# Attention worked off by pairs of steps, with one sum over the first two pairs of a region and GpSimd scaling 99 of 128 blocks

## What is computed

```python
q = (query @ Wq + bq).reshape(Bq, Sq, H, DK)      # Bq = 8, Sq = Sk = 512, H = 16, DK = 16
k = (key @ Wk + bk).reshape(Bq, Sk, H, DK)
v = (value @ Wv + bv).reshape(Bq, Sk, H, DK)
scores = jnp.einsum('bqhd,bkhd->hbqk', q, k) / np.sqrt(DK)
attn = jax.nn.softmax(scores.reshape(H * Bq, Sq, Sk), axis=0).reshape(H, Bq, Sq, Sk)
out = jnp.einsum('hbqk,bkhd->bqhd', attn, v).reshape(Bq, Sq, H * DK)
x = x + jnp.tanh(g_xattn[0]) * (out @ Wo + bo)
x = x + jnp.tanh(g_ffn[0]) * ffn(layernorm(x))
```

## Time and profile before

| what | value |
| --- | --- |
| time, median of 3 runs | 893.19 us (891.55 to 894.06) |
| time of the profiled execution | 890.11 us |
| its span, first to last instruction | 888.3 us |
| mean granted TensorE clock | 0.973 of 2.4 GHz |
| PE busy | 770.7 us (87%) |
| DVE busy | 781.0 us (88%) |
| ACT busy | 706.7 us (80%) |
| POOL busy | 494.9 us (56%) |
| `attend` | about 312 to 743 us |

### The profile page before, as it was taken

One profiled execution on the slowest core, in us unless ns is written; L12 is line 12 of the kernel. 1 busy time (PEld: TensorE's weight loads), 2 busy tenths in 40 slices (PEclk: granted clock), 3 DMA queues, 4 the chain that ended last, 5 costly groups with the idle time before them and its releaser, 6 DMA issues. The chain is left out here.

```text
span 888.3 us, 20668 instructions
## 1 busy us (share of the span) xinstructions
PE 770.7 (87%) x8127; PEld 438.8 (49%) x8149; DVE 781.0 (88%) x1001; ACT 706.7 (80%) x1095; POOL 494.9 (56%) x353
## 2 busy tenths in 40 slices
PE   8897887877777688999889999999999989948977
PEld 6563361112212155666556666666666657714434
DVE  4799539999999979999799999999999995767968
ACT  3454449999999878899788999999999952768973
POOL 1333463000000017999898999999999996514500
PEclk9999999999999989999999999999999989969999
DMA  9796786565555567778776786768857566200014
GB/s 299 262 315 203 245 240 130 138 167 140 140 139 130 202 183 228 239 225 265 231 227 211 234 265 191 212 174 259 259 164 211 168 225 192 91 1 1 0 43 148
DMA packets 98094, 164.34 MB, mean 185 GB/s; under 512 B 9616, under 2 KB 37008, under 8 KB 97680
## 3 DMA queue, kind: packets, MB, share of 16 engines
q1 hardware_dynamic: 98000, 163.03, 61.5%
HBM read 133.63 MB, written 41.94 MB: 198 GB/s over the span
## 5 line engine op out<-in xcount | busy, mean ns | idle before, releaser
L978 POOL TENSOR_TENSOR e<-e,recip 128x768 f32<-128x768 f32 (+3 forms) x256 | 387.4, 1558 | 34.6 <-DVE recip L1020 34.6
L928 ACT ACTIVATE e<-ps_att 128x512 f32<-128x512 f32 x512 | 302.0, 648 | 36.6 <-PE ps_att L869 35.6
L1009 DVE TENSOR_REDUCE pair_sums<-e 128x128 f32<-128x2048 f32 x128 | 291.6, 2281 | 20.0 <-ACT e L928 19.6
L869 PE MATMUL ps_att<-arena 128*128 128x128 bf16 x2048 | 192.7, 220 | 0.3 <-issue 0.2
L884 PE MATMUL acc<-e,arena 128*32 128x128 f32 x4096 | 179.5, 294 | 11.7 <-DVE e L990 4.2
L869 PEld LDWEIGHTS ps_att<-arena 128*128 128x128 bf16 x2048 | 151.0, 98 | 58.8 <-issue 3.6
L694 ACT ACTIVATE copies<-ps_max 128x1024 bf16<-128x1024 f32 x189 | 175.6, 1087 | 0.0
L865 PE MATMUL ps_att<-shift,minus 128*128 128x512 bf16 x394 | 154.2, 391 | 14.9 <-DMA arena<-k_stack 9.2
L884 PEld LDWEIGHTS acc<-e,arena 128*32 128x32 f32 x4096 | 106.6, 111 | 40.7 <-POOL e L978 10.9
L709 DVE TENSOR_TENSOR high<-copies,high 128x3072 bf16<-128x3072 bf16 x63 | 110.0, 1745 | 0.4 <-ACT copies L694 0.4
L961 POOL CAST bo_parts<-arena 96x256 bf16<-96x256 f32 x1 | 0.4, 394 | 175.5 <-DMA arena<-in_L_xattn_bo_dram 175.5
(11 more groups left out here) (162 smaller groups left out, 879.0 us busy)
## 6 DMA issues: line engine op xcount, KB each, us to landing
arena<-k_stack SPq DMA_DIRECT2D x256, 256.0 KB, 3.3
arena<-q_stack SPq DMA_DIRECT2D x64, 256.0 KB, 4.2
k_stack<-parts SPq DMA_DIRECT2D x40, 256.0 KB, 3.5
q_stack<-parts SPq DMA_DIRECT2D x40, 256.0 KB, 3.6
k_stack<-k_stack SPq DMA_DIRECT2D x12, 512.0 KB, 10.9
arena<-in_x_dram SPq DMA_DIRECT2D x5, 1024.0 KB, 8.7
arena<-in_ctx_dram SPq DMA_DIRECT2D x4, 1024.0 KB, 6.5
arena<-q_stack SPq DMA_DIRECT2D x8, 512.0 KB, 8.0
```

The costliest lines, as they stand in the source:

```text
L869: last = nc.tensor.matmul(bank[:, j * P:(j + 1) * P], ks[:, i % KRING, b * P:(b + 1) * P], qs[:, h, b * P:(b + 1) * P], start=False, stop= ...
L928: nc.scalar.activation(e_at(qc * STEPS + i, half * HB, (half + 1) * HB).rearrange("p q b i -> p b q i"), ps[(qc * (2 * STEPS) + 2 * i + ha ...
L978: nc.gpsimd.tensor_tensor(part, part, by_pairs(recip[:, kc % 2, :], share), ALU.mult).then_inc(pool_scaled, 1)
L1009: nc.vector.tensor_reduce(pair_sums[:, :, h // 2, :], e[:, g % RING // 2].rearrange("p q s b i -> p q i (s b)"), AX.X, ALU.add).then_inc(s ...
```

## The change

All lists of `attend` except SyncE's now go by pairs. PE computes the four halves of scores of a pair and then the product of both steps of the pair 10 before it. Before, the product of one step stood behind every two halves. The ring has 11 slots of a pair, which is the same memory. DVE sums pairs 0 and 1 of a region with one instruction, unless the two do not lie beside each other in the ring, and each other pair with one; it adds up seven partial sums. DVE and GpSimd each scale a whole pair with one instruction. GpSimd takes 9, 13, 13, 13, 13, 12, 13, 13 of the 16 blocks of the eight pairs, 99 of 128, and 6 of 16 in the last region. DVE scales a pair 8 pairs after its sum's place in the list. The gathers stand behind pairs 4, 6, 8 and 10 of a chunk of queries.

```diff
-    LAG = 20
-    SLAG = 17
-    RING = 22
+    LAG = 10
+    RING = 11
+    GATHER_AT = [LAG - PAIRS + BANK_PAIRS * (j + 1) for j in range(BANKS)]
-        return 7 if i % 4 == 1 else 6
+    POOL_BLOCKS = (9, 13, 13, 13, 13, 12, 13, 13)
+    END_BLOCKS = 6
+    GROUPS = ((0, 1), (2,), (3,), (4,), (5,), (6,), (7,))
...
 TensorE
-                    for i in range(STEPS):
-                        for half in range(2):
-                            scores(qc, i, half)
-                        if LAG <= i < LAG + H and (i - LAG) % BANK_HEADS == 0:
...
-                        if i >= LAG or not first:
-                            for half in range(2):
-                                times_v(qc * STEPS + i - LAG, half)
+                    for j in range(CHUNK):
+                        for half in range(4):
+                            scores(qc, 2 * j + half // 2, half % 2)
+                        if LAG <= j < LAG + PAIRS and (j - LAG) % BANK_PAIRS == 0:
+                            bank = (j - LAG) // BANK_PAIRS
+                            if not first:
+                                pe.wait_ge(gathered, BANKS * (qc - 1) + bank + 1)
+                            clear(bank)
+                        if j >= LAG or not first:
+                            times_v(qc * CHUNK + j - LAG)
...
 ScalarE
+                        if p >= RING:
+                            act.wait_ge(multiplied, p - RING + 1)
+                        for half in range(4):
+                            n = 4 * p + half
+                            act.wait_ge(scored, n + 1)
...
 GpSimd
+                for p in range(ALL_PAIRS):
+                    r = p // PAIRS
+                    if p % PAIRS == 0:
+                        pool.wait_ge(recip_ready, r + 1)
+                    share = pool_share(p)
+                    part = e_at(p, 0, share)
+                    nc.gpsimd.tensor_tensor(part, part, by_pairs(recip[:, r % 2, :], share), ALU.mult
+                                            ).then_inc(pool_scaled, 1)
...
 VectorE
+                def add_up(p, n, k):
+                    dve.wait_ge(exped, 4 * (p + n))
+                    t = p % RING
+                    nc.vector.tensor_reduce(partial[:, :, k, :], e[:, t:t + n].rearrange("p t q z i -> p q i t z"),
+                                            AX.XY, ALU.add).then_inc(sum_done, 1)
...
+                for r in range(NC * NC):
+                    for k, (p, n) in enumerate(groups(r)):
+                        if r:
+                            if k == 0:
+                                dve.wait_ge(sum_done, groups_before(r) + r)
+                            if p % PAIRS < PAIRS - 1:
+                                for i in range(n):
+                                    scale(p + i - PAIRS)
+                                if p % PAIRS + n == PAIRS - 1:
+                                    scale(p + n - PAIRS)
+                        add_up(p, n, k)
+                    invert(r, len(list(groups(r))))
+                for p in range(ALL_PAIRS - PAIRS, ALL_PAIRS):
+                    scale(p)
```

More of the change, by code:

```diff
@@ L746, in attend, with pool_share, groups, groups_before @@
     STORE_AT = 26
-    GATHER_AT = [LAG - H + BANK_HEADS * (j + 1) + 2 for j in range(BANKS)]
+    BANK_PAIRS = BANK_HEADS // 2
+    GATHER_AT = [LAG - PAIRS + BANK_PAIRS * (j + 1) for j in range(BANKS)]
     Q_STEPS = {STEPS - H + h + 2 * h // 3: h for h in range(H)}
[L751 to L755, removed]
-        return 7 if i % 4 == 1 else 6
-    FIRST_PRESET = 2 * LAG + 3
+    POOL_BLOCKS = (9, 13, 13, 13, 13, 12, 13, 13)
+    END_BLOCKS = 6
+    GROUPS = ((0, 1), (2,), (3,), (4,), (5,), (6,), (7,))
+    def pool_share(p):
+        return END_BLOCKS if p >= ALL_PAIRS - PAIRS else POOL_BLOCKS[p % PAIRS]
+    def groups(r):
+        for group in GROUPS:
+            p = r * PAIRS + group[0]
+            if len(group) == 2 and p % RING == RING - 1:
+                yield p, 1
+                yield p + 1, 1
+            else:
+                yield p, len(group)
+    def groups_before(r):
+        return sum(len(list(groups(i))) for i in range(r))
+    FIRST_PRESET = 4 * LAG + 3
     def preset(n):
@@ L872, in scores, with times_v @@
                     last.then_inc(scored, 1)
[L874 to L888, removed]
+                def times_v(p):
+                    pe.wait_ge(pool_scaled, p + 1)
+                    pe.wait_ge(dve_scaled, p + 1)
+                    kc, pair = p % CHUNK // PAIRS, p % PAIRS
+                    for odd in range(2):
+                        for b in range(B):
+                            col = (pair * 2 + b // HB) * P
+                            grp = 32 * (b % HB)
+                            v_col = pair * 3 * DK + DK * odd
+                            z = odd * B + b
+                            last = nc.tensor.matmul(acc[grp:grp + 32, col:col + P], vpad[:, kc, b, v_col:v_col + 32],
+                                                    e_at(p, z, z + 1), start=False, stop=False,
+                                                    skip_group_check=True)
+                    last.then_inc(multiplied, 1)
                 def clear(j):
@@ L909, in _ @@
                     chunk(qc, False)
-                for g in range(ALL - LAG, ALL):
-                    for half in range(2):
-                        times_v(g, half)
+                for p in range(ALL_PAIRS - LAG, ALL_PAIRS):
+                    times_v(p)
             @block.scalar
@@ L921, in chunk @@
                 def chunk(qc, first):
[L922 to L927, removed]
-                            nc.scalar.activation(
[L929 to L933, removed]
+                    for j in range(CHUNK):
+                        p = qc * CHUNK + j
+                        if p >= RING:
[3 more added lines that the diff above has]
+                            act.wait_ge(scored, n + 1)
+                            nc.scalar.activation(
+                                e_at(p, half * HB, (half + 1) * HB).rearrange("p q z i -> p z q i"),
+                                ps[n % SCORES][:].rearrange("p (z q i) -> p z q i", z=HB, i=2),
+                                ACT.Exp, scale=DK ** -0.5).then_inc(exped, 1)
                             if preset(n + SCORES):
@@ L936, in chunk @@
                                 nc.scalar.activation(ps[n % SCORES][:].rearrange("p (b q) -> p b q", q=P),
-                                                     shift_at(qc, (i + 1) // H).to_broadcast([P, HB, P]), ACT.Copy,
+                                                     shift_at(qc, j // PAIRS).to_broadcast([P, HB, P]), ACT.Copy,
                                                      scale=-1.0).then_inc(shift_set, 1)
-                        if i in GATHER_AT and not first:
-                            if i == GATHER_AT[0]:
+                        if j in GATHER_AT and not first:
+                            if j == GATHER_AT[0]:
                                 if qc >= 2:
@@ L969, in _ @@
                 split_bias()
[L971 to L979, removed]
@@ L984, in _ @@
             @block.vector
             def _(dve):
[L986 to L990, removed]
-                                            ALU.mult).then_inc(dve_scaled, 1)
[L993 to L1029, removed]
+                def scale(p):
+                    r = p // PAIRS
+                    if p % PAIRS == 0:
+                        dve.wait_ge(recip_copied, r + 1)
+                    share = pool_share(p)
+                    part = e_at(p, share, BLOCKS)
+                    nc.vector.tensor_tensor(part, part, by_pairs(recip_v[:, (r % 2) * P:(r % 2 + 1) * P], BLOCKS - share),
+                                            ALU.mult).then_inc(dve_scaled, 1)
@@ new lines, in add_up, with invert @@
+                def add_up(p, n, k):
[3 more added lines that the diff above has]
+                                            AX.XY, ALU.add).then_inc(sum_done, 1)
+                def invert(r, n):
+                    done = groups_before(r + 1) + r
+                    dve.wait_ge(sum_done, done)
+                    nc.vector.tensor_reduce(summed[:].rearrange("p (q i) -> p q i", i=2),
+                                            partial[:, :, 0:n, :].rearrange("p q k i -> p q i k"), AX.X, ALU.add
+                                            ).then_inc(sum_done, 1)
+                    dve.wait_ge(sum_done, done + 1)
+                    if r >= 2:
+                        dve.wait_ge(pool_scaled, (r - 1) * PAIRS)
+                    nc.vector.reciprocal(recip[:, r % 2, :], summed[:]).then_inc(recip_ready, 1)
+                    dve.wait_ge(recip_ready, r + 1)
+                    nc.vector.tensor_copy(recip_v[:, (r % 2) * P:(r % 2 + 1) * P], recip[:, r % 2, :]
+                                          ).then_inc(recip_copied, 1)
```

22 lines of the change are left out of this document (9 added, 13 removed).

## The result

The changed kernel takes 933.99 us (933.48 to 936.14) against 892.54 us, the median of four runs of before: 1.0465 times the time of before, with an interval of 1.0444 to 1.0486. The forecast was 936.5. The profiled execution took 933.85 us, where 933.5 was forecast.

What follows compares the result with a forecast made beforehand. PE, ACT and three score banks bound `attend` by a 3.14 us cycle, growing to 3.56: 344.8 + 116 x 3.56 + 4.5 + 3 = 765.3 against 721.9; median 893.2 + 43.3 = 936.5 us, range 918 to 962.

Steps and rivals of the forecast that it cites:

- The ring as the bound: In `attend`, the cycle shift, last scores and product, next scores, exponential, next shift sets a pair's period: 3.14 us before.
- ACT's 112 waits: ACT's waits for PE's scores in `attend` before the change, one for each pair of steps, 35.4 us in all.
- One drain for two products: PE's two adjacent products pay the idle time of a width change once, so the second adds 0.42 us.
- The ring's length, 3.56: New period of a pair in `attend`: 1.06 + 0.62 + 0.42 + 0.72 + 0.74 = 3.56 us, against 3.14.
- The second product: PE's product directly behind the first, ahead of the next scores, adds 0.42 us to each pair's period.
- the step from the exponential to the shift: Time on ACT from the start of its exponential to the start of the next shift: 0.74 us.
- ACT's wait: ACT's wait for PE in each pair grows to 0.20 + 0.42 = 0.6 us, 70 us in all, hiding the gathers.
- `clear` and key loads: PE's `clear` matmuls add 15 x 0.3 = 4.5 us; stalls for late keys shrink from 9 to 3 us.
- Start: First product of `attend` moves from 340.27 to 342.3; the next shift follows 2.5 us later, at 344.8.
- clock rival: PE's idle time drops the granted clock to 1.2 GHz for stretches: 965 us and more, chance 0.04.
- The tail: End of `attend`: shorter GpSimd list against a last product one step longer (0.42), about -0.1 us, counted as nothing.
- The shorter lists: DVE's list falls from 24.8 to 24.3 us in a region, GpSimd's from 25.7 to 23.5.

Runs made afterwards that it cites:

- the run with two changes: Changed kernel with the first step's product behind the second half of scores and the second step's behind the third: 891.68 us, 0.9994 of before.
- the old lists with the free order: Kernel before, with the two products of a pair of steps behind the second and third half of scores: 893.89 us, 1.0020 of before.
- the version with both products ahead: Changed kernel with both products moved behind the third half of scores, ahead of the fourth: 884.75 us, 0.9933 of before.

## Why the prediction was right

- **The ring as the bound.** Right for the changed kernel: two runs that move nothing but PE's order reproduce the loss and undo it. ACT's 112 waits were the sign that mattered; the busy shares were not. For the kernel before it is half the truth. DVE's list was as long as the ring, so that cutting the ring alone gained nothing.
- **One drain for two products.** Right. The change of width is paid once: 32 or 48 weight loads, one idle time of 0.22. The rule of the Trainium skill (TensorEngine Tiling (Array Packing), Key Properties) that a change of the tiling mode drains the array fits this and the run with two changes.
- **The ring's length, 3.56.** Right as a sum (3.57 measured), by two errors that cancel, which is luck. The second product costs 0.49 instead of 0.42, and the step from the exponential to the shift takes 0.66 instead of 0.74. Why that step became shorter was not tested.
- **ACT's wait.** It rose to 0.65 us in the pair shown and 87.0 us in all (0.6 and 70 forecast; the 87.0 include 4.9 at the start of the stage and other waits outside the ring). The gathers did hide in it: the pair with the gather at 561.61 has a period of 3.58.
- **`clear` and key loads.** 3.75 to 3.8 instead of 3.57 in the pairs with a clear, so 0.2 each where 0.3 was taken; keys 2.5 instead of 3. Together they are 2 us, and the last shift came 2.0 us earlier than forecast, counted from the start of the stage.
- **Start.** The first product came at 341.75, 28.4 us after the stage's first matmul, against 27.4 before: 1.0 later, where 2.0 was forecast. But the granted clock stood at 0.50 from 340.9 to 347.7 us, so that the next shift came 3.7 us after the product instead of 2.5 and the period behind it was 4.22 us long instead of 3.56: 1.8 us, which took that gain back and more. I had worked out a clock rival for the ring and not for this one wait.
- **The tail.** From the last shift to the last gather 20.2 us against 20.5: nothing, as worked out.
- **After `attend`.** From the last product to the end it was 2.1 us longer in the profiled run, though nothing there was changed. The granted clock goes with it. The windows behind the last product (columns as above), before and changed:

```profile
742.10:888.30 146.20, 116.49 (x626) 68.08 (x621) 104.63 (x212) 98.79 (x150) 46.69 (x41) 0.93 0.20 65
783.70:932.00 148.30, 119.06 (x631) 68.81 (x621) 104.69 (x212) 98.85 (x150) 46.65 (x41) 0.92 0.20 64
```

PE alone is busy for longer, 119.1 against 116.5 us, and the clock stands at 1.2 GHz for 24.4 us of the stretch against 20.0, by the clock records of the traces. The traces of the ten experiments agree: with 20.0 to 20.6 us at 1.2 GHz this stretch takes 146.1 to 146.5 us, with 24.3 or 24.4 it takes 148.4 to 148.7, with 27.6 to 27.9 it takes 148.9 to 149.6. So the match of 933.5 with 933.85 for the profiled execution is luck in part: these 2.1 us and 0.5 in the stages in front, neither of them forecast, made up for the 2.0 us by which the last shift came early.
- **The shorter lists.** The gain of DVE, 0.5 us in a region, was right in size (24.6 where DVE sets the pace, against 25.1 to 25.9 in the regions without late keys of the old lists with the free order) and off the path in the changed kernel.

What was mis-sized stood in the expectations of the runs. Behind the ring I named GpSimd at 25.4 us for a region as the old lists' bound, where PE waited for DVE and the region took 25.2, and I left out that a faster PE asks for keys sooner.

## What to carry to other kernels

When an engine with an in-order list shares a few buffers with another, look for the wait that comes once in each period and add up the ring around it from start to start. Work placed just behind a wait is hidden or not by where it stands, not by how long it is: here 0.5 us of matmuls cost 4.6% behind the fourth half of scores, and nothing like it ahead of it. Before a list is shortened, ask whether a ring of the same length stands beside it: here cutting the one or the other gained nothing clear, and cutting both gained 0.7% in one order of PE and nothing in the other. The next bound (here the key loads) has to be looked for then.

## What the runs showed of the hardware that I had not expected

Products in 32-column groups on float32, from the start of the first to the next scores, take 0.63, 1.12 and 1.61 us for one, two and three: 0.49 for each further one. Key loads of 256 KB, with a median of 3.3 us to land (3.5 in the version with both products ahead), kept PE waiting 18.8 us instead of 9.2 when the median period fell from 3.14 to 2.99 us, though each is issued two pairs ahead. And the granted clock stood at 1.2 GHz for 6.8 us around a wait of 2.62 us on PE, for 3.4 us around waits of 0.55 and 1.04 us, and not at all around one of 2.09: the rows show what it costs, not when it falls.
